# A two-layer attention and feed-forward kernel on one Trainium2 core: one pool of eight banks, attention work of the first layer in three stretches per unit, and another order and rotation in the second

## The reference, cut to what matters

```python
def attn0(x, Wq, Wk, Wv, Wo):            # 32 query heads, 8 key/value heads of 16, 4 batches of 256 rows
    attn = softmax(einsum('bhqd,bhkd->bhqk', q, k) * 0.25)
    return (attn @ v) @ Wo.T
def ffn0(x, W1, b1, W2, b2):             # 512 -> 2048 -> 512
    return gelu(x @ W1 + b1) @ W2 + b2
def attn1(x, w_qkv, b_qkv, w_dense, b_dense):   # the same heads; q and k are turned by _rope, causal mask
    rot = concatenate([-x2, x1], axis=-1)       # x1, x2: the two halves of the 16 numbers of a head
    q = q * cos + rot * sin
    return softmax(where(mask, q k^T / 16, min)) @ v @ w_dense.T + b_dense
def ffn1(x, w12, b12, w3, b3):           # 512 -> 2 * 512 -> 512
    return (silu(x1) * x2) @ w3.T + b3
xn = layernorm(x); x = x + attn0(xn) + ffn0(xn)
xn = layernorm(x); x = x + attn1(xn) + ffn1(xn)
```

## Time and profile before

| | us |
|---|---|
| median of 3 runs | 584.15 (583.16 to 585.2) |
| the profiled execution, device time | 581.91 |
| its span, first to last instruction | 580.1 |
| TensorE busy in it | 554.5 (96%) |
| DVE, ACT, POOL busy | 449.2, 338.5, 242.9 |
| granted TensorE clock, mean | 0.997 of full speed |

### The profile page before, as it was taken

How to read it: one execution, slowest core, us unless ns; L and a number is a source line. 1 busy time by engine, 2 the same in 40 slices (tenths; PEclk the granted TensorE clock), 3 DMA queues, 4 the chain that set the end, 5 groups by cost and what they waited for, 6 DMA issues and landing times.

```text
span 580.1 us, 10527 instructions
## 1 busy us (share of the span) xinstructions
PE 554.5 (96%) x3216; PEld 405.0 (70%) x3216; DVE 449.2 (77%) x1232; ACT 338.5 (58%) x595; POOL 242.9 (42%) x353
## 2 busy tenths in 40 slices
PE   3999999999999999999999999999899999989997
PEld 3876667776776776766676677767677877766754
DVE  6496887666786695678898587989998998698673
ACT  3548775666377556567746655466645664574551
POOL 6332325730342531214323116655743675364242
PEclk9999999999999999999999999999999999998999
DMA  6368433344233235224244314344433344355001
GB/s 200 114 207 236 139 117 92 102 129 122 60 96 105 65 101 129 70 68 149 98 137 146 92 38 147 74 133 141 112 93 109 93 113 132 105 146 128 4 14 61
DMA packets 30983, 64.02 MB, mean 110 GB/s; under 512 B 5744, under 2 KB 18288, under 8 KB 29904
## 3 DMA queue, kind: packets, MB, share of 16 engines
q1 hardware_dynamic: 22288, 35.03, 21.6%
q0 software_dynamic: 8640, 28.32, 16.3%
HBM read 48.64 MB, written 13.24 MB: 107 GB/s over the span
## 4 chain that ended last, share of the span: by engine, by line
PE 74%; DVE 11%; issue 5%; POOL 4%; DMA 3%; ACT 2%; SPq 0%; DVEq 0%; POOLq 0%; ACTq 0%
PE banks L901 52%; PE banks L1032 7%; PE banks L999 4%; PE banks L1011 3%; PE banks L978 3%; PE banks L960 3%; DVE banks L1310 2%; DMA q_all<-max_t 1%; DMA x_res<-in_x 1%; PE banks L921 1%; POOL probs L827 1%; DVE neg_max L1318 1%; DVE x_res L1357 1%; DVE w_up L1198 1%; DVE hid L1378 1%
## 5 line engine op out<-in xcount | busy, mean ns | idle before, releaser
L1142 ACT ACTIVATE probs<-banks 128x512 f32<-128x512 f32 (+1 forms) x256 | 131.4, 544 | 151.0 <-PE banks L999 75.3
L901 PE MATMUL banks<-xnT,w_up 128*128 128x512 f32 x576 | 151.2, 403 | 0.0
L1318 DVE TENSOR_REDUCE neg_max<-banks 128x2 f32<-128x512 f32 x128 | 82.1, 683 | 64.1 <-PE banks L960 63.7
L901 PE MATMUL banks<-w_down,hid 128*128 128x512 f32 x480 | 126.7, 401 | 0.2
L901 PEld LDWEIGHTS banks<-xnT,w_up 128*128 128x128 f32 x576 | 102.2, 189 | 34.0 <-DVE neg_max L1318 9.2
L1310 DVE CUSTOM_DVE_ANT_0 banks<-banks,mask_qk 128x128 f32<-128x128 f32 (+1 forms) x256 | 86.3, 374 | 28.8 <-PE banks L978 28.4
L901 PEld LDWEIGHTS banks<-w_down,hid 128*128 128x128 f32 x480 | 86.1, 188 | 27.5 <-issue 7.4
L827 POOL TENSOR_SCALAR_AFFINE_SELECT probs<-probs 128x256 f32<-128x256 f32 x128 | 60.6, 474 | 71.9 <-ACT probs L1142 64.9
L901 PE MATMUL banks<-xnT,w_qkv 128*128 128x256 f32 x576 | 80.6, 290 | 1.8 <-DVE xnT L1254 1.4
L901 PEld LDWEIGHTS banks<-xnT,w_qkv 128*128 128x128 f32 x576 | 74.0, 194 | 6.5 <-DVE xnT L1254 1.8
L1357 DVE TENSOR_TENSOR x_res<-x_res,banks 128x512 f32<-128x512 f32 x96 | 63.5, 676 | 10.4 <-PE banks L901 10.2
(11 more groups left out here) (83 smaller groups left out, 727.9 us busy)
## 6 DMA issues: line engine op xcount, KB each, us to landing
...
```

The source lines that it names most:

```text
L901: mm = nc.tensor.matmul(out_ap, lhs(a), rhs(b_), start=first and j == 0, stop=stop and j == 2, **kw)
L1142: nc.scalar.activation(probs[:, i, 0:w], banks[:, ST_BANKS[i % 2], 0:w], ACT.Exp, scale=SCALES[n // B]).then_inc(exp_done, 1)
L1318: nc.vector.tensor_reduce(neg_max[:, s, at:at + 2, t], banks[:, bank_of[x][a], :].rearrange("p (r t) -> p r t", r=2), AX.X, ALU.max, negat ...
```

## The change

**First layer.** The slots of a unit hold attention work at three places (`STRETCHES`): slot 0 has two steps of `st` and one of `m`, slot 3 the same, slot 6 has two steps of `m` and both steps of `pv`. Before, slots 0, 2, 4 and 6 had one `st` and one `m` each, and a `pv` stood in slot 0 (of the unit before) and in slot 4. `norm` and `ctx` move accordingly, `qkv` and `wo` go ahead of `up` in the fill, the splits of the `up` weights go from slot 4 to slot 6, adds stand first in their slot, and `opening` puts one part of a dense piece ahead of a stretch. The weights of `spread` give slots 6 and 7 more dense work.

**Banks.** In the first layer all eight banks form one pool, `st` and `pv` included; in the second `st` keeps banks 0 and 1 and `pv` bank 6. A step gets the bank that an estimate of the readers' times (`readers`) says is free first.

**Second layer.** `mt` (slot 5) and `pv` stand ahead of that slot's `m`; what DVE has to do for earlier steps stands ahead of the slot's `m` too (`head` leaves `m` out from unit 18 on).

**Rotation.** The rows of the query weights are laid out so that the two halves of a head lie in two column blocks of `qkv_v` on the same partitions. DVE's two products are then 128 partitions by 256 instead of 64 by 512. The table has a third column block, and a store takes 64 partitions with four rows each instead of 128 with two.

```diff
+STRETCHES = (0, 3, 6)
+BANKS = 8
...
-        head = [k for k, x in enumerate(slot) if x[0] in ("st", "m", "mt", "mrow")]
+        head = [k for k, x in enumerate(slot) if x[0] in ("st", "mt", "mrow") or x[0] == "m" and x[1] < LU + 2]
         cut = head[-1] + 1 if head else 0
-        for x in slot[:cut] + due[g] + slot[cut:]:
+        early = [x for x in due[g] if x[0] == "add" and x[1] == 0]
+        first = opening(slot, o, due[g]) if any(x[0] == "st" and x[1] < LU for x in slot[:cut]) else []
+        slot = first + [x for x in slot if x not in first]
+        cut += len(first)
+        for x in early + slot[:cut] + [x for x in due[g] if x not in early] + slot[cut:]:
...
-        elif i % 2 == 0:
-            slots[i].append(("st", u, i // 2))
+        elif i in STRETCHES[:2]:
+            j = 2 * STRETCHES.index(i)
+            slots[i] += [("st", u, j), ("st", u, j + 1)]
...
-            if i in (2, 4, 6):
-                slots[i].append(("m", u + 2, i // 2 - 1))
+            if i == STRETCHES[1]:
+                slots[i].append(("m", u + 2, 0))
+            if i == STRETCHES[2]:
+                slots[i] += [("m", u + 2, 1), ("m", u + 2, 2)]
...
+    if u < LU:
+        slots[STRETCHES[2]] += [("pv", u, 0), ("pv", u, 1)]
+        slots[7].append(("norm", u, 0))
+    else:
+        slots[5].append(("pv", u, 0))
...
+    if L == 1:
+        x = slots[5]
+        slots[5] = [y for y in x if y[0] != "m"] + [y for y in x if y[0] == "m"]
...
+def banks_for(x, layer):
+    if x[0] == "st" and layer == 2:
+        return ST_BANKS
+    if x[0] == "pv" and layer == 2:
+        return (PV_BANK,)
+    return [k for k in range(BANKS) if layer == 1 or k not in ST_BANKS and k != PV_BANK]
...
-                k = [k for k in recent if k not in taken][0]
-                recent.remove(k)
-                recent.append(k)
+                k = min((k for k in banks_for(x, phase) if k not in taken), key=lambda k: free_at[k])
+                now = max(now, free_at[k]) if phase else now
                 if k in user:
                     before[x].append(user[k])
...
-                    nc.vector.tensor_tensor(rot_b[0:64, 0:w, :], qkv_v[64:P, 0:w, :],
-                                            other[64:P].to_broadcast([64, w, T]), ALU.mult).then_inc(rot_sin, 1)
-                    nc.vector.tensor_tensor(rot_b[64:P, 0:w, :], qkv_v[0:64, 0:w, :],
-                                            other[0:64].to_broadcast([64, w, T]), ALU.mult).then_inc(rot_sin, 1)
+                    if w == 2:
+                        for j in range(2):
+                            nc.vector.tensor_tensor(rot_b[:, j, :], qkv_v[:, 1 - j, :], table[:, 1 + j, :],
+                                                    ALU.mult).then_inc(rot_sin, 1)
```

192 lines of the change are left out of this document (120 added, 72 removed).

## The result

The changed kernel takes 585.46 us in the median of 20 runs (581.42 to 588.08), the kernel before 583.62 us (20 runs beside them, 581.18 to 585.53): a ratio of 1.0033, 95% interval 1.0017 to 1.0048. It is slower by 1.8 us where 7 us less were forecast. The profiled execution took 583.44 us with a span of 581.5, against 581.91 and 580.1 before.

The account below looks back on a forecast made before the run. TensorE bounds the kernel, 554.5 of 580.1 us busy; the second layer also has waits. First layer -4.0 and second -3.0 us make 584.15 - 7.0 = 577.2 us; forecast 573.5 to 580.5, range 571.0 to 584.5.

Parts of the forecast that it names:

- both sums: Net forecasts by layer: first layer -8.5 + 4.5 = -4.0 us, second layer -3.0 us after giving back 0.9.
- Shape changes: First layer, TensorE: 188 changes of array shape for 242, at 0.20 or 0.12 us each; -8.5 us.
- New waits for banks: First layer: stretches want six banks at once, so TensorE waits 6.0 us more; present waits of 1.5 may go; net 4.5.
- The three reused banks: Units 11, 12, 15: second `st` gets the bank the first just filled; 0.85 us plus 0.2 for `m`, 3.2 in all.
- The first `pv`: Units 1, 2, 6, 10: it takes the bank of the `down` just ahead; 0.2 to 0.4 us each, 1.0 in all.
- The `m` behind two `st`: Slot 0, nine units: takes a `down` bank, waits if DVE is late (units 10 to 13); 1.8 us with units 0, 14, 15.
- Rival C: Slower: first-layer bank waits become the rule, DVE later by bunched maxima, 1.0 us in each of 16 units; 588.7 us, chance 0.12.
- the text's own signs for being wrong: `st` behind `st` 0.43 us apart, first-layer waits for ACT or DVE over 8 us, or DVE's busy time not falling 6 us.
- Row of maxima: Second layer: the row comes 0.8 us earlier ahead of `m`, saving 2.2 of 2.7 us; nothing where a store holds the queue.
- Waits for exponentials: Second layer: `m` between `pv` and the next `st` gives ACT 0.23 us more each time, 5 waits; -0.7 us.
- Rotation: Second layer: shorter products save 7.5 us of DVE, counted as -1.0 us; store costed at nothing; port sharing might cancel it.
- rival B: Little reaches the end: new waits 6.5 us, second layer brings nothing; 582.2 us, chance 0.18.

Follow-up runs that it names:

- pool_waits_hid: Changed kernel plus one wait: in the first layer GpSimd's subtraction for the next `up` weights waits for DVE's second `hid` subtraction of the unit; 582.89 us.
- up7_maxima_first: Changed kernel with the first layer's `up` casts in slot 7, not 6, and both second-layer order edits undone, rotation by columns kept; 577.67 us.
- up_slot7: Changed kernel with one number altered: the first layer's casts and low part of the next `up` weights in slot 7, not 6; 580.89 us.
- up7_l0_only: Changed kernel with the first layer's `up` casts in slot 7, not 6, and both second-layer order edits and the rotation undone; 579.12 us.
- up7_halves: Changed kernel with the first layer's `up` casts in slot 7, not 6, and only the rotation undone (queries turned by halves); 581.17 us.
- l0_only: Changed kernel with the second layer's order and the rotation put back as in the kernel before; 583.85 us.
- l1_only: Kernel before with only the second layer's order edits and the rotation by columns; 583.04 us.
- the better kernel: Changed kernel with the first layer's `up` casts in slot 7, not 6, and the second layer's slot 5 as before (`m` ahead of `mt` and `pv`); 576.50 us.

## Why the prediction was wrong, by its steps

In the two traces the first layer ends where it did (-4.0 us forecast, 0.0 measured), and the rest of the span is 1.5 us longer (-3.0 forecast). So both sums failed, by 4.0 and 4.5 us.

**Shape changes, -8.5 us: right.** TensorE's busy time fell by 9.4, and the traces have 188 changes for 242. A stretch in unit 8 of the changed kernel:

```profile
196.44 0.73 PE L1079 MATMUL banks<-q_all,k_sb 49*128 49x512 f32 x4
197.01 0.40 PE L1041 MATMUL banks<-k_sb,q_all 48*128 48x256 f32 x4
197.34 2.77 PE L982 MATMUL banks<-xnT,w_qkv 128*128 128x256 f32 x21
```

Two `st` in 0.57 us and the `m` in 0.33, as forecast (0.34 + 0.23 + 0.34): `st` behind `st` pays nothing. The Trainium skill (TensorEngine Tiling (Array Packing), Key Properties), which the prediction weighed, says that a change of tiling mode, not of tile, drains TensorE, and the trace agrees.

**New waits for banks, +6.0 less 1.5: mis-sized, the step that failed in the first layer.** The waits are 9.0 us against 0.8, 8.2 net for 4.5 forecast; of the 1.5 us that might go only 0.8 were there. The three reused banks were sized well: the second `st` of units 11, 12 and 15 begins 0.95 us late each time, 0.78 of it idle (1.05 forecast with the `m`; by the prediction's own numbers, 0.54 + 0.60 - 0.34, its 0.85 is 0.80). The first `pv` waits in the four units that it named, 1.5 us for 1.0. The `m` behind two `st` waits 2.8 us in units 2, 3, 4, 6, 9 and 13, for 1.8 that were put mostly on others. The bank of `pv` costs 0.7 us and four smaller rows 1.6, and no term stood for them.

I had taken DVE's durations as given. The only overlap of DVE with GpSimd that I weighed was that of the rotation; I never asked where 32 `hid` subtractions would lie once 2.48 us of maxima stood ahead of them and the casts of `up` in slot 6. Without the collision the waits of `m` for additions are 0.7 us and the kernel is 2.6 us faster (`pool_waits_hid`), so it explains a part of the miss and not all: 7.2 us of waits stay. Rival C had the mechanism, DVE later in each unit by the bunching in slot 6, but laid it on the maxima themselves, and it bit in six of 16 units. Of the text's own signs for being wrong, waits of `m` or `st` for ACT or DVE of over 8 us did not come (they are 5.9 us, 7.4 with `pv`); a DVE whose busy time did not fall by 6 us did, as it rose by 8.2.

**Row of maxima, -2.2 us: its wait right, what it is worth wrong.** The order does shorten the wait: 6.1 to 3.9 us with the rotation by columns (`up7_maxima_first`, `up_slot7`), 2.0 to 1.0 with that by halves (`up7_l0_only`, `up7_halves`). In the changed kernel it rose all the same, from 2.7 to 4.1 us, since the rotation's stores add more than that. The prediction had the condition (nothing is won where a store holds the queue) and priced it at no gain, not at a loss. The half of the order that does not shorten the wait, slot 5, costs 1.9 us here and 4.4 in the better kernel.

**Waits for exponentials, -0.7: right, and larger** (2.9 to 1.6 us).

**Rotation, -1.0: its size right, its worth wrong, the step that failed in the second layer.** The busy time of all products went from 20.2 to 12.7 us, the 7.5 us forecast, at 511 ns each. "The store is costed at nothing" is the step: it lands 0.9 us later, and the waits for the row grow by 2.9 us (`up7_halves` to `up_slot7`) or 4.1 (`up7_l0_only` to `up7_maxima_first`). In the time the two rotations can't be told apart. The Trainium skill's rule on the shared port pair (SBUF — State Buffer), which the prediction held only against these products, agrees with the `hid` rows in that an operation with two SBUF inputs is held while GpSimd's runs. The prediction gave it 1 us, for the rotation; in the first layer the same held-up subtractions cost 2.6 us.

**Keys, not in the sum at all.** The two waits for keys are 2.6 us longer than before. The one for GpSimd's fill of `k_sb`, at the layer boundary, comes with the first layer's order (1.5 us in `l0_only` too, 0.6 in `l1_only`). The other is 0.8 us in `l0_only` and 1.0 in `l1_only`, so each layer's edits bring some of it.

**The clock: not in the sum at all.** 1.1 to 1.5 of the 1.8 us.

The range ended at 584.5 us, between rival B and rival C, and the time is 585.46.
